# Attention stage of a convolution, attention and expert kernel: projections ahead of the next transposes, logits one quad later, exponential last, the key turned early

## What is computed

```
x = x + W2( abs(lowpass(gelu(x W1 + b1))) ) + b2          # per image
q, k, v = ln(x) Wq + bq, ln(x) Wk + bk, ln(x) Wv + bv     # 12 heads share k and v, 16 wide
q, k = rotary(q), rotary(k)
x = x + softmax(q . k * scale) v                          # each token with itself alone
logits = ln(x) gate                                       # 8 experts, best 2 of them
x = x + sum over the 2 experts of p_e * down_e(silu(gate_e(ln x)) * up_e(ln x))
```

## Time and profile before

| | |
|---|---|
| median of 3 runs | 494.07 us (493.1 to 494.08) |
| the profiled execution's own time | 497.88 us |
| its span, first to last instruction | 496.1 us |
| TensorE busy (matmuls) | 398.8 us, 80% |
| VectorE | 289.8 us, 58% |
| GpSimd | 269.0 us, 54% |
| ScalarE | 207.6 us, 42% |
| attention, from its first instruction to its last copy of logits | 72.9 to 196.4 us |
| mean granted clock of TensorE | 0.871 of full speed |

### The profile page before, as it was taken

One profiled execution on the slowest core, in us unless ns is written; L12 is line 12 of the kernel. 1 busy time (PEld: TensorE's weight loads), 2 busy tenths in 40 slices (PEclk: granted clock), 3 DMA queues, 4 the chain that ended last, 5 costly groups with the idle time before them and its releaser, 6 DMA issues.

```text
span 496.1 us, 9117 instructions
## 1 busy us (share of the span) xinstructions
PE 398.8 (80%) x2236; PEld 373.0 (75%) x2237; DVE 289.8 (58%) x748; ACT 207.6 (42%) x481; POOL 269.0 (54%) x281
## 2 busy tenths in 40 slices
PE   5799938468887667156799999999999999998950
PEld 5799926457776556056699999999989989998850
DVE  1266572688877771997266666654555556454630
ACT  3434512323333211065355555555545545554530
POOL 0155560655555530001646787878878788786753
PEclk9999999867777655555699999999999999999995
DMA  7979512003343322200323344444434444443432
GB/s 215 254 202 237 152 16 91 24 29 109 95 119 104 109 76 87 35 1 1 109 40 47 69 75 64 71 74 67 73 67 75 76 61 72 72 70 54 66 38 27
DMA packets 46436, 41.23 MB, mean 83 GB/s; under 512 B 14121, under 2 KB 40524, under 8 KB 46412
## 3 DMA queue, kind: packets, MB, share of 16 engines
q0 software_dynamic: 13824, 16.82, 21.4%
q1 hardware_dynamic: 32588, 24.14, 18.3%
HBM read 25.87 MB, written 15.08 MB: 83 GB/s over the span
## 4 chain that ended last, share of the span: by engine, by line
POOL 21%; issue 15%; DMA 12%; PE 2%; SPq 1%; POOLq 0%; ACT 0%; DVE 0%; ACTq 0%
DMA out<-moe_y,idx_map 12%; POOL out L1069 11%; POOL moe_xt L1061 10%; SPq L1306 1%; DMA moe_xt<-rows,idx_map 1%; POOLq L1054 0%; PE moe_ps_gt L1103 0%; PE moe_ps_x L1094 0%; PE moe_ps_y L1128 0%; PE moe_ps_gt L1104 0%; PE moe_ps_gt L1107 0%; PE moe_ps_gt L1105 0%; PE moe_ps_gt L1106 0%; PE moe_ps_x L1095 0%; PE moe_ps_h L1114 0%
## 5 line engine op out<-in xcount | busy, mean ns | idle before, releaser
L1069 POOL DMA_INDIRECT out<-moe_y,idx_map x72 | 114.2, 1587 | 50.4 <-SPq L1317 25.4
L1061 POOL DMA_INDIRECT moe_xt<-rows,idx_map x72 | 71.3, 990 | 58.7 <-issue 58.7
L1267 DVE TENSOR_TENSOR moe_y<-moe_yy 128x192 f32<-128x192 f32 x72 | 25.9, 360 | 88.0 <-DMA out<-moe_y,idx_map 71.8
L1204 ACT ACTIVATE moe_yy<-moe_ps_y,moe_xt 128x384 f32<-128x384 f32 x72 | 41.9, 582 | 72.1 <-PE moe_ps_y L1128 72.1
L1128 PE MATMUL moe_ps_y<-wd,moe_h_hi 128*128 x216 | 71.4, 356 | 0.6 <-DVE moe_h_lo L1259 0.6
L1184 ACT ACTIVATE moe_x_hi<-moe_ps_x 128x256 fp32r<-128x256 f32 x72 | 27.6, 383 | 46.7 <-PE moe_ps_x L1095 46.7
L1128 PEld LDWEIGHTS moe_ps_y<-wd,moe_h_hi 128*128 128x128 f32 x216 | 40.9, 189 | 2.3 <-issue 2.2
L1259 DVE TENSOR_TENSOR moe_h_lo<-moe_ps_h,moe_h_hi 128x384 fp32r<-128x384 f32 x72 | 40.2, 558 | 3.1 <-ACT moe_h_hi L1196 0.9
L1253 DVE TENSOR_TENSOR moe_hid<-moe_ps_u,moe_sg 128x384 f32<-128x384 f32 x72 | 39.5, 548 | 1.2 <-ACT moe_sg L1190 1.2
L1130 PE MATMUL moe_ps_y<-wd,moe_h_lo 128*128 x144 | 36.2, 252 | 0.0
L1196 ACT ACTIVATE moe_h_hi<-moe_ps_h 128x384 fp32r<-128x384 f32 x72 | 35.4, 492 | 1.2 <-PE moe_ps_h L1114 1.2
(11 more groups left out here) (182 smaller groups left out, 1144.7 us busy)
## 6 DMA issues: line engine op xcount, KB each, us to landing
xs<-in_x SPq DMA_DIRECT2D x8, 384.0 KB, 5.8
conv_stage<-in_wgu SPq DMA_DIRECT2D x8, 384.0 KB, 3.9
conv_stage<-in_wgu SPq DMA_DIRECT2D x16, 192.0 KB, 4.8
rows<-attn_xr SPq DMA_DIRECT2D x8, 384.0 KB, 2.7
out<-xs SPq DMA_DIRECT2D x8, 384.0 KB, 3.4
attn_stage<-in_down SPq DMA_DIRECT2D x8, 288.0 KB, 3.3
conv_xta<-in_xT SPq DMA_DIRECT2D x8, 256.0 KB, 4.5
moe_xt<-rows,idx_map POOLq DMA_INDIRECT x72, 2.8
```

Source lines behind the costliest of these rows:

```text
L1061: nc.gpsimd.indirect_dma_start(xt[:, slot, :], None, rows.ap(), bass.IndirectOffsetOnAxis(ap=idx_map[:, j, 0:1], axis=0)).then_inc(gathere ...
L1069: nc.gpsimd.indirect_dma_start(out, bass.IndirectOffsetOnAxis(ap=idx_map[:, j, 1:2], axis=0), y[:, j % YR, :], None, compute_op=ALU.add).t ...
L1204: nc.scalar.activation(yy[:, s].rearrange("p h c -> p (h c)"), ps_y[:, s, 0:2 * C], ACT.Copy, scale=xt[:, slot, bass.ds(GC + e, 1)]).then_ ...
```

## The change

TensorE and ScalarE work through passes n = 0 to 11, all written out. TensorE's pass: products(n) (projections if n < 8, logits of quad n-4 if n >= 4), turn(n+1), turn_route(n-3). Before it was turn(n+1), turn_route(n-3), products(n) with the logits of n-3. ScalarE's pass: copy_products(n), out_of_psum(n+1), route_out_of_psum(n-3), split(n), exponential(n). Before it was out_of_psum(n+1), route_out_of_psum(n-3), copy_products(n), split(n), exponential(n). GpSimd's pass: rotate_key(n+1), deviation(n-1), weigh_value(n), split(n+1). Before it was rotate_key(n), split(n), deviation(n-1), weigh_value(n), with all but the first two quads in a loop. VectorE and SyncE are as before, VectorE still in its loop.

```diff
@@ -37,6 +37,7 @@
 QUADS = TILES // QT
 HT, HR = 2, 4
 LAG = 3
+LAG_OUT = LAG + 1
 RING = 2
 XR = 12
 AHEAD = XR - 2
@@ -597,7 +598,7 @@
                             nc.tensor.matmul(at, xa[:, s, bass.ts(t, P)], wqa[:], start=True, stop=False)
                             ins = nc.tensor.matmul(at, xb[:, s, bass.ts(t, P)], wqb[:], start=False, stop=True)
                     if route:
-                        pe.wait_ge(rev_done, made(q - LAG))
+                        pe.wait_ge(rev_done, made(q - LAG_OUT))
                         for t in range(QT):
                             at = ps_q[:, s, 0, ps_lg.start + t * EXPERTS:ps_lg.start + (t + 1) * EXPERTS]
                             nc.tensor.matmul(at, ra[:, bass.ts(t, P)], ga[:], start=True, stop=False)
@@ -605,17 +606,12 @@
                     ins.then_inc(qkv_done, 1)
 
                 turn(0, 0)
-                for n in range(LAG):
-                    turn(*turned(0, n + 1))
-                    products(*turned(0, n), route=False)
-                with pe.Fori(LAG // RING, last) as i:
-                    for r in range(1, 1 + RING):
-                        turn(*turned(i, r + 1))
-                        turn_route(*turned(i, r - LAG))
-                        products(*turned(i, r))
-                for n in range(QUADS - 1, QUADS + LAG):
-                    turn_route(*turned(0, n - LAG))
-                    products(*turned(0, n), project=n < QUADS)
+                for n in range(QUADS + LAG_OUT):
+                    products(*turned(0, n), project=n < QUADS, route=n >= LAG_OUT)
+                    if n + 1 < QUADS:
+                        turn(*turned(0, n + 1))
+                    if 0 <= n - LAG < QUADS:
+                        turn_route(*turned(0, n - LAG))
 
             @block.scalar
             def _(act):
@@ -648,7 +644,7 @@
                             ins = nc.scalar.activation(qkv[:, s, 2 * h:2 * h + 2, :],
                                                        ps_q[:, s, h, 0:2 * QW].rearrange("p (t c) -> p t c", t=2), ACT.Copy)
                     if route:
-                        ins = nc.scalar.activation(lg[:, bass.ts(q - LAG, QT), :],
+                        ins = nc.scalar.activation(lg[:, bass.ts(q - LAG_OUT, QT), :],
                                                    ps_q[:, s, 0, ps_lg].rearrange("p (t e) -> p t e", t=QT), ACT.Copy)
                     ins.then_inc(cp_done, 1)
 
@@ -662,26 +658,17 @@
                     nc.scalar.activation(wd[:, quad(i, s), :, 0, :], stage[:, s].rearrange("p (k c) -> p k c", k=3),
                                          ACT.Copy).then_inc(hi_done, 1)
 
-                def attend(i, s):
-                    split(i, s)
-                    exponential(i, s)
-
                 out_of_psum(0, 0)
-                for n in range(LAG):
-                    out_of_psum(*turned(0, n + 1))
-                    copy_products(*turned(0, n), route=False)
-                    attend(*turned(0, n))
-                with act.Fori(LAG // RING, last) as i:
-                    for r in range(1, 1 + RING):
-                        out_of_psum(*turned(i, r + 1))
-                        route_out_of_psum(*turned(i, r - LAG))
-                        copy_products(*turned(i, r))
-                        attend(*turned(i, r))
-                for n in range(QUADS - 1, QUADS + LAG):
-                    route_out_of_psum(*turned(0, n - LAG))
-                    copy_products(*turned(0, n), project=n < QUADS)
+                for n in range(QUADS + LAG_OUT):
+                    copy_products(*turned(0, n), project=n < QUADS, route=n >= LAG_OUT)
+                    if n + 1 < QUADS:
+                        out_of_psum(*turned(0, n + 1))
+                    if 0 <= n - LAG < QUADS:
+                        route_out_of_psum(*turned(0, n - LAG))
                     if n < QUADS:
-                        attend(*turned(0, n))
+                        split(*turned(0, n))
+                    if n < QUADS:
+                        exponential(*turned(0, n))
 
             @block.gpsimd
             def _(pool):
@@ -732,17 +719,14 @@
 
                 rotate_key(0, 0)
                 split(0, 0)
-                weigh_value(0, 0)
-                rotate_key(0, 1)
-                split(0, 1)
-                deviation(0, 0)
-                weigh_value(0, 1)
-                with pool.Fori(1, QUADS // RING) as i:
-                    for s in range(RING):
-                        rotate_key(i, s)
-                        split(i, s)
-                        deviation(i - 1 + s, 1 - s)
-                        weigh_value(i, s)
+                for n in range(QUADS):
+                    if n + 1 < QUADS:
+                        rotate_key(*turned(0, n + 1))
+                    if n:
+                        deviation(*turned(0, n - 1))
+                    weigh_value(*turned(0, n))
+                    if n + 1 < QUADS:
+                        split(*turned(0, n + 1))
                 deviation(last, 1)
 
             @block.vector
```

## The result

The changed kernel takes 491.14 us (median of 20 runs, 488.55 to 495.12) where the kernel before takes 494.60 (20 runs). The ratio is 0.9936, 95% interval 0.9917 to 0.9955: 3.2 us less, 2.2 to 4.1 (the two medians by themselves differ by 3.5). The forecast was 490.8 from 494.07, 3.3 less.

The account below looks back on a forecast made before the run. No engine alone bounds the kernel; in attention, engines hand work on in two equally long rings. Savings 0.95+1.62+1.1-0.4 = 3.3 us, from 494.07 to 490.8; own range 489.3 to 492.3, with rivals 487.2 to 495.0.

Parts of the forecast that it names:

- The two rings: Attention's loops of waits: VectorE with GpSimd, and ScalarE's exponential and copies with TensorE's logits; 12.15 us a turn.
- (a): Start of attention: TensorE projects quad 0 before turning quad 1; 0.95 us saved, bounds 0.67 and 1.73.
- if that switch keeps its place in time: At the start, TensorE's matmul groups turn from 0.80 to 0.41 us near 84.4, unmoved by their earlier begin.
- (b): First step, quad 0 to 1: earlier copy of projections and earlier key give 7.15 for 8.77 us, 1.62 saved.
- (c): Six later attention turns: copy waits for the residual, deviation follows the key; 71.7 for 72.88 us, 1.1 saved.
- the lock holds in full: Rival, chance 0.05: in attention `attn_xr` waits out both GpSimd weighings, 2.89 us; 4.0 us lost, 494.8, no change.
- the prediction's own sign: Stated test in attention: the forecast is wrong where `attn_xr` behind rstd takes something other than 2.2 us.
- the two-port case: In attention, VectorE in a two-port mode and GpSimd share a port pair; by the page in full, 4 us worse.
- (d): End of attention: logits lag four quads, one more pass; tail stays 25.3 us, 4.2 more if not covered.
- (e): Loops of TensorE, ScalarE and GpSimd written out, with their instruction fetching: costs nothing, bounds 0.5 us either way.
- (f): TensorE's projections and logits in attention's turns: 7.8 us fit into 9.7; 0.4 us lost for products(2).
- the cold rival: Chance 0.12: TensorE's clock stays low in attention, products with logits take 10.6 for 9.7; 5.8 us lost, 496.2.

Follow-up runs that it names:

- The better GpSimd order: GpSimd in the order deviation, key, weighing, split: 494.31 us put into the kernel before, 482.41 us put into the changed kernel.

## Why the prediction was right, and where its terms were off

**Bound and rings.** The two rings are shown by pairs of runs. The better GpSimd order gains nothing under the old rest (494.31) and 12 us under the new one (482.41). For the change's own GpSimd order the picture is less clean: it costs 24 us under the old rest, and under the new one it wins in the first step alone, as the old GpSimd order has turns of 11.75 to 12.12 there.

**(a) the start, 0.95.** Mis-sized. From the first `attn_xn` to T(0) the old order took 15.32 and 13.79 in the two profiles of before, and 14.60 and 15.27 in the two variants that keep it; 14.75 on the mean. The new order in eight profiles took 13.37 to 14.83, mean 14.51. That is 0.2 us for 0.95, within a scatter of 1.5. The one profile that the 0.95 was worked from had the longest start of the old order. The step that failed is "if that switch keeps its place in time". First the changed kernel:

```profile
77.66 1.14 PE L598 MATMUL attn_ps_q<-wqa,attn_xa 128*128 128x240 f32 x2 [1.25 <-ACT attn_xb L629]
...
80.99 0.73 PE L598 MATMUL attn_ps_q<-wqa,attn_xa 128*128 128x240 f32 x2
```

Then the last of the eight groups in the variant with the new TensorE and ScalarE order and the old GpSimd order, where they began at 78.56:

```profile
84.30 1.01 PE L599 MATMUL attn_ps_q<-wqb,attn_xb 65*128 65x240 f32 x2
```

The groups turned short 3.6 us behind their first one in the first profile of the changed kernel. In the variant, in the second profile of the changed kernel and in three more of the eight none did.

**(b) the first step, 1.62.** Exact: 8.77 to 7.14 and 7.16. Its condition, products(1) in time, held in eight of nine profiles with the new order on TensorE and GpSimd's key ahead, not in the one with the split held back, whose first step took 9.73.

**(c) the turns, 1.1.** The chain of waits was right, item by item: copy behind the residual, key, deviation, `attn_xr`, turns of 11.6 to 11.9. Two lengths in it were wrong, and they nearly cancel. The prediction took the product's 2.21 in the earlier trace rows for its own length; it is 1.01, and the rest waits for GpSimd's split (1.40). So the residual ends at T+3.2, not 4.33. In the kernel before, the split starts just ahead of the product at 159.34:

```profile
159.26 1.40 POOL L714 TENSOR_TENSOR wd<-attn_stage,wd 128x576 f32 x1
```

The first of the product's two instructions ended at 161.07, 0.41 behind the split, after 1.74 us; the second took 0.55.

In the changed kernel the split follows weighing and lies on `attn_xr`, which takes 3.14, not 2.23. The prediction had asked of the split only who waits for its result, and called it covered; it costs 1.08. Beside the weighings alone `attn_xr` took 2.06, near the forecast 2.23 and under the 2.89 of the rival "the lock holds in full". So that rival had its size wrong, and its price for the whole, no gain, too, since the product had become free. By the prediction's own sign (`attn_xr` other than 2.2) this step was wrong, and the turn came out by luck.

From the end of one product to the end of the last, the six turns took 72.87 before and 72.25 and 71.49 after: 0.6 and 1.4 less, for 1.1. Against the second profile of before, 76.52, it is 4.3 and 5.0. And the half without the new GpSimd order had 71.56, so what these turns gained was there with TensorE's and ScalarE's new order alone. The key turned early added nothing to it, against the prediction's sum.

The section Who interferes with whom of the SBUF — State Buffer page of the Trainium skill also has a VectorE instruction with two SBUF inputs contend with a GpSimd instruction that reads SBUF, and one with at most one SBUF input not, unless it runs in a two-port mode. The traces agree: 1.01 against 2.2 to 2.3 for the product, 0.95 against 2.00 for the residual, and an unchanged 0.95 for the reduction. The normalisation reads one tensor and is stretched all the same, 1.25 to 3.14, which fits the two-port case that the prediction named for it. The prediction weighed the rule for `attn_xr` alone and missed that it already stood in the product's row.

**(d) the tail, 25.3.** Unchanged: from the end of the last product 23.1 in both (173.29 to 196.39, 168.16 to 191.26). **(e)** No cost seen.

**(f) TensorE, 0.4.** In the first profile after, the products of quad 7 ran wholly at the lower clock:

```profile
148.16 1.14 PE L598 MATMUL attn_ps_q<-wqa,attn_xa 128*128 128x240 f32 x2 [2.88 <-ACT attn_xb L629]
...
154.70 0.43 PE L604 MATMUL attn_ps_q<-ga,attn_ra 128*128 128x8 f32 x2
...
158.20 0.59 PE L605 MATMUL attn_ps_q<-gb,attn_rb 64*128 64x8 f32 x2
...
158.83 1.03 ACT L644 ACTIVATE attn_qkv<-attn_ps_q 128x480 f32<-128x480 f32 x2 [2.03 <-PE attn_ps_q L605]
```

148.16 to 158.7 is 10.5 us, as the cold rival had it (10.6 for 9.7), and the step 6-7 was 12.87, 1.3 late. It happened in one turn of six, not in all; 1.3 and 0.6 us in one profile and 1.1 in one turn of the other are more than the 0.4 of the sum. What the prediction did not price is the other side. The kernel before pays for the same slow stretches, with no such slack; its second profile lost 4 us in two turns. How the 3.2 us divide between shorter waits and this stays open; the two profiles of each kernel (attention 122.3 and 124.4, after it 118.2 and 118.8) are too few to tell.

The sum came out, 3.3 for 3.2, and only in part for the reasons given. Term (b) was right. Term (a) was 0.7 too large, the turn held one length 1.2 too long and one 0.9 too short, and TensorE's slow stretches cost both kernels more than was priced. That these went against each other is luck.

## What to carry to other kernels

Before a duration in a row is used as an instruction's own, compare it with the same instruction beside an idle GpSimd: here 2.21 of the product held 1.2 of waiting, and moving the GpSimd work moved the wait. Ask of each moved instruction what it comes to lie beside, and not only who waits for it. Put GpSimd's work beside VectorE instructions that it does not stretch (here the reduction and the row statistics, not the normalisation, though that too reads one tensor), and order a helper's queue by what the ring wants first (deviation before key); the two together took off another 13 us, four times what the change did. A reordering in one queue can cost 24 us alone, and another can bring nothing alone and 12 us with its partner, so test the halves.

## Unexpected of the hardware

TensorE's clock made turns of one and the same kernel differ by up to 3 us (12.27 and 15.03 side by side in the second profile of before, granted clock 0.72 on the mean of the turns), and a start by 1.5. GpSimd and VectorE stretch each other: the product 1.01 to 2.30, four normalisations 1.25 alone, 1.6 beside the key, 2.06 beside weighing, 3.14 beside weighing and split; on the other side two weighings 1.64 to 1.96 and the split 1.40 to 1.72.
